# Expert sums straight from PSUM on VectorE, and inverse roots from ScalarE and VectorE instead of GpSimd's powers

## The reference

```
weights = softmax over the two best of x @ expert_embeddings.T
first 512 tokens of each expert's list are kept (capacity)
inter = relu(tokens_e @ first_linear[e].T)      # 512 x 256 -> 512 x 512
out   = inter @ second_linear[e].T * weight     # 512 x 512 -> 512 x 256
x     = layernorm(x + sum of both experts' out)
```

## Time and profile before

| | us |
|---|---|
| median of 3 runs (lowest, highest) | 1020.33 (1018.7, 1022.15) |
| the profiled execution's own time | 1013.04 |
| its span, first to last instruction | 1010.9 |
| PE busy in the span | 980.9 (97%) |
| DVE, ACT, POOL busy | 823.5, 724.2, 587.9 |

### The profile page before, as it was taken

How to read it: one execution, slowest core, us unless ns; L and a number is a source line. 1 busy time by engine, 2 the same in 40 slices (tenths; PEclk the granted TensorE clock), 3 DMA queues, 4 the chain that set the end, 5 groups by cost and what they waited for, 6 DMA issues and landing times.

```text
span 1010.9 us, 21647 instructions
## 1 busy us (share of the span) xinstructions
PE 980.9 (97%) x7018; PEld 928.6 (92%) x7018; DVE 823.5 (81%) x2087; ACT 724.2 (72%) x1857; POOL 587.9 (58%) x1069
## 2 busy tenths in 40 slices
PE   8999999999999999999999999999999999999993
PEld 6789999999999999999999999999999999889993
DVE  6887878888888888887888788878888887767774
ACT  6686877777787768786878677877777766547761
POOL 4743465665566656665575637565665464536786
PEclk9999999999999999999999999999999999999997
DMA  7663031112211131104110402031112213555542
GB/s 249 193 143 109 16 110 47 51 46 88 69 52 46 59 98 52 47 18 140 51 46 2 135 29 58 33 110 47 51 46 91 98 31 124 193 173 163 170 149 88
DMA packets 63030, 88.97 MB, mean 88 GB/s; under 512 B 15540, under 2 KB 44008, under 8 KB 62920
## 3 DMA queue, kind: packets, MB, share of 16 engines
q1 hardware_dynamic: 56968, 71.10, 22.8%
q0 software_dynamic: 5952, 16.50, 4.9%
HBM read 49.31 MB, written 38.26 MB: 87 GB/s over the span
## 4 chain that ended last, share of the span: by engine, by line
PE 79%; ACT 6%; DVE 6%; issue 4%; POOL 2%; DMA 1%; POOLq 0%; SPq 0%; DVEq 0%; ACTq 0%
PE ps L629 21%; PE ps L631 21%; PE ps L630 21%; PE ps L658 7%; PE ps L737 3%; DVE nmx L1838 2%; PE ps L673 1%; PE ps L675 1%; PE ps L775 1%; ACT hp L1094 1%; PE ps L768 1%; ACT prob L1251 1%; POOL out L2327 1%; PE ps L761 1%; DMA cxs<-in_ctxt 1%
## 5 line engine op out<-in xcount | busy, mean ns | idle before, releaser
L2212 POOL TENSOR_SCALAR prob<-prob,rinv 128x333 f32<-128x333 f32 x256 | 143.5, 572 | 234.5 <-DVE rinv L1847 234.0
L1246 ACT ACTIVATE oT_hi<-ps 128x256 fp32r<-128x256 f32 x126 | 48.4, 384 | 150.5 <-PE ps L675 150.5
L629 PE MATMUL ps<-kv_lo,w_hi 128*128 128x256 f32 (+1 forms) x512 | 154.9, 303 | 1.1 <-DVE kv_lo L1398 1.1
L631 PE MATMUL ps<-kv_hi,w_hi 128*128 128x256 f32 (+1 forms) x512 | 152.9, 299 | 0.0
L630 PE MATMUL ps<-kv_hi,w_lo 128*128 128x256 f32 (+1 forms) x512 | 152.5, 298 | 0.0
L1251 ACT ACTIVATE prob<-ps,nmx 128x333 f32<-128x333 f32 x256 | 134.8, 537 | 7.7 <-DVE nmx L1838 7.7
L1398 DVE TENSOR_TENSOR pT_lo<-ps,pT_hi 128x512 fp32r<-128x512 f32 x254 | 130.8, 549 | 0.9 <-ACT pT_hi L1263 0.3
L1838 DVE TENSOR_REDUCE nmx<-ps 128x2 f32<-128x666 f32 x128 | 108.4, 847 | 8.4 <-PE ps L631 7.0
L658 PE MATMUL ps<-ident,prob 128*128 128x128 f32 (+1 forms) x768 | 105.9, 273 | 1.8 <-POOL prob L2212 1.0
L629 PEld LDWEIGHTS ps<-kv_lo,w_hi 128*128 128x128 f32 x512 | 96.9, 189 | 1.7 <-issue 1.5
L631 PEld LDWEIGHTS ps<-kv_hi,w_hi 128*128 128x128 f32 x512 | 96.8, 189 | 0.0
(11 more groups left out here) (330 smaller groups left out, 3319.3 us busy)
## 6 DMA issues: line engine op xcount, KB each, us to landing
wraw<-in_W SPq DMA_DIRECT2D x14, 512.0 KB, 5.2
vcd_hi<-vst_hi SPq DMA_DIRECT2D x10, 512.0 KB, 2.7
vcd_lo<-vst_lo SPq DMA_DIRECT2D x10, 512.0 KB, 3.7
v_hi<-vcd_hi SPq DMA_DIRECT2D x32, 154.0 KB
v_lo<-vcd_hi SPq DMA_DIRECT2D x32, 154.0 KB
slots<-initr SPq DMA_DIRECT2D x8, 522.0 KB, 9.9
xs<-in_x SPq DMA_DIRECT2D x16, 256.0 KB, 4.3
xts<-in_xT SPq DMA_DIRECT2D x15, 256.0 KB, 4.0
```

Source lines behind the costliest of these rows:

```text
L629: pe.matmul(dst, hi1, lo2, start=first, stop=False, skip_group_check=True)
L631: return pe.matmul(dst, hi1, hi2, start=False, stop=last, skip_group_check=True)
L2212: pool.tensor_scalar(prob[:, h % 2, t, 0:KEYS], prob[:, h % 2, t, 0:KEYS], rinv[:, h % 2, t:t + 1], 1.0, ALU.mult, ALU.mult).then_inc(norm ...
```

## The change

1. The inverse roots of the expert norms leave POOL (`power` is gone). ACT takes a square root (`deviation`), DVE its reciprocal and one Newton step (`inverse`: four instructions, each of which waits for the one before). One Sqrt on a scratch tile is put at the end of ACT's `ending()`.
2. The results no longer pass through ACT (`result`, `result_tile` are gone): DVE reads PSUM, multiplies by the slot's weight and adds `bs` in one instruction a tile (`sum_of`); `z_set` counts tiles instead of halves, and PE waits for it in place of `yo_set` before it writes a bank again.
3. In ACT's loop `scale(e - 1)` stands in one piece, and `deviation` ahead of the fourth `relu` tile.
4. `block_moments` moves from ahead of `part1(1, 1)` to behind `weights(1, 1, 16)`, and `block_norm` from ahead of `xparts(1)` to behind `shift(0)` in the first round of the loop. SP's program keeps its order.
5. For the last sequence's norm POOL's power has 2 columns in place of 4, and DVE leaves out two small instructions (`residual_stats` returns early).

```diff
@@ sync
-                    keep_sums(e, slice(0, 2), 2 * e + 1)
-                    keep_sums(e, slice(2, 4), 2 * e + 2)
+                    keep_sums(e, slice(0, 2), 4 * e + 2)
+                    keep_sums(e, slice(2, 4), 4 * e + 4)
@@ tensor: outer, outer_tiles, last_outer
-                    need(pe, yo_set, 4 * e - 2 + 2 * pair)
+                    need(pe, z_set, 4 * e - 2 + 2 * pair)
@@ scalar
                 xparts(0)
+                act.activation(warm[:], warm[:], ACT.Sqrt)
...
+            def deviation(part, e, tiles):
+                act.wait_ge(fstat_set, 3 * part + 3)
+                act.activation(f_sd[:, e, tiles], f_vv[:, e, tiles], ACT.Sqrt).then_inc(fsd_set, 1)
...
-            result(0, 0, (0, 1))
             xparts(1)
-            result(0, 0, (2, 3))
             for e in range(1, E - 1):
                 u = e % 2
                 parts(e + 1, 1 - u)
-                relu(e)
+                relu(e, range(0, 3))
+                deviation(e - 1, e - 1, slice(0, ST))
+                relu(e, range(3, 4))
                 xparts(e + 1)
-                scale(e - 1, (0, 1), e - 1)
-                if e < E - 2:
-                    result(e, u, (0, 1))
-                    scale(e - 1, (2, 3), e - 1)
-                    result(e, u, (2, 3))
...
+                scale(e - 1, range(ST), e - 1)
...
             last_relu(1, (0, 1))
+            deviation(E - 2, E - 2, slice(0, 3))
+            deviation(E - 1, E - 2, slice(3, 4))
             scale(E - 2, T_ORDER[0:3], E - 2)
             scale(E - 2, T_ORDER[3:4], E - 1)
             last_relu(1, (2, 3))
+            deviation(E, E - 1, slice(0, 2))
+            deviation(E + 1, E - 1, slice(2, 4))
@@ vector
                 dve.tensor_scalar(c_vv[:, 0, :], c_mv[:, :, 1], 1.0, EPS, ALU.mult, ALU.add).then_inc(cstat_set, 1)
+                if at(b, B):
+                    return
...
+            def sum_of(e, s, bank):
+                u = e % 2
+                need(dve, z_st, PART + 32 * (e - 1))
+                need(dve, fo_set, 4 * (e - 1))
+                base_of(e, s // 2)
+                return dve.scalar_tensor_tensor(out=yo[u][:, s, :], in0=bank, scalar=wsl[:, e, s:s + 1],
+                                                in1=bs[u][:, s, 0:D], op0=ALU.mult, op1=ALU.add).then_inc(z_set, 1)
             def sums(e, half):
-                dve.wait_ge(yo_set, 4 * e + 2 * half + 2)
-                base_of(e, half)
-                dve.tensor_tensor(yo[u][:, o, :], yo[u][:, o, :], bs[u][:, o, 0:D], ALU.add).then_inc(z_set, 1)
+                dve.wait_ge(o_mm, 2 * e + half + 1)
+                dve.wait_ge(cols_set, 3 * e + 3)
+                for s in (2 * half, 2 * half + 1):
+                    sum_of(e, s, ps[:, 6 + half, (s % 2) * D:(s % 2 + 1) * D])
...
+            def inverse(part, e, tiles, steps):
+                o = (slice(None), e, tiles)
+                dve.wait_ge(fsd_set, part + 1)
+                dve.reciprocal(f_r0[o], f_sd[o]).then_inc(fnm_set, 1)
+                dve.wait_ge(fnm_set, steps + 1)
+                dve.scalar_tensor_tensor(out=f_cr[o], in0=f_r0[o], scalar=-0.5, in1=f_r0[o], op0=ALU.mult,
+                                         op1=ALU.mult).then_inc(fnm_set, 1)
+                dve.wait_ge(fnm_set, steps + 2)
+                dve.tensor_tensor(f_cr[o], f_cr[o], f_vv[o], ALU.mult).then_inc(fnm_set, 1)
+                dve.wait_ge(fnm_set, steps + 3)
+                dve.scalar_tensor_tensor(out=f_rs[o], in0=f_cr[o], scalar=1.5, in1=f_r0[o], op0=ALU.add,
+                                         op1=ALU.mult).then_inc(fnm_set, 1)
+                dve.wait_ge(fnm_set, steps + 4)
             def shift(part, e, tiles):
-                dve.wait_ge(frs_set, part + 1)
+                inverse(part, e, tiles, 5 * part)
...
             relu(0)
-            block_moments()
             part1(1, 1)
             dve.wait_ge(sc_done, 64 * B)
             part2(1, 1)
-            block_norm()
             xparts(1)
             weights(1, 1, 16)
+            block_moments()
             sums(0, 0)
             for e in range(1, E - 1):
...
                 shift(e - 1, e - 1, slice(0, ST))
+                if e == 1:
+                    block_norm()
                 xparts(e + 1)
@@ gpsimd
-                pool.wait_ge(cstat_set, 7 * B)
-                pool.tensor_tensor(c_rs[:].rearrange("p c t -> p (c t)"), c_vv[:].rearrange("p c t -> p (c t)"), powm[:],
-                                   ALU.pow).then_inc(crs_set, 1)
+                pool.wait_ge(cstat_set, 7 * B - 2)
+                pool.tensor_tensor(c_rs[:, 0, :], c_vv[:, 0, :], powm[:, 0:NT], ALU.pow).then_inc(crs_set, 1)
...
             for e in range(1, E - 1):
-                power(e - 1, e - 1, slice(0, ST))
                 gather(e)
                 finished(e - 1, range(ST))
-            power(E - 2, E - 2, slice(0, 3))
-            power(E - 1, E - 2, slice(3, 4))
             gather(E - 1)
-            finished(E - 2, (0, 1, 2), T_ORDER)
-            power(E, E - 1, slice(0, 2))
-            finished(E - 2, (3,), T_ORDER)
-            power(E + 1, E - 1, slice(2, 4))
+            finished(E - 2, range(ST), T_ORDER)
             finished(E - 1, range(ST))
```

More of the change, by code:

```diff
@@ L280, in build @@
         f_vv = s2("f_vv", [P, E, ST])
+        f_sd = s2("f_sd", [P, E, ST])
+        f_r0 = s2("f_r0", [P, E, ST])
+        f_cr = s2("f_cr", [P, E, ST])
         f_rs = s2("f_rs", [P, E, ST])
@@ L1009, in outer_tiles @@
                 for n, s in enumerate(T_ORDER):
-                    need(pe, yo_set, (4 * e - 2, 4 * e, 4 * e + 1, 4 * e + 2)[n])
+                    need(pe, z_set, (4 * e - 2, 4 * e, 4 * e + 1, 4 * e + 2)[n])
                     for i in range(I // P):
@@ L1043, in last_outer @@
                 if s < 2:
-                    need(pe, yo_set, 4 * e - 2 + 2 * s)
+                    need(pe, z_set, 4 * e - 2 + 2 * s)
                 for i in tiles:
@@ L1321, in _, with relu @@
             ending()
-            def relu(e):
-                for i in range(I // P):
+            def relu(e, tiles=range(I // P)):
+                for i in tiles:
                     need(act, h_mm, 4 * stage(e) + i + 1)
@@ L1328, in relu @@
                     act.activation(h_hi[:, i, :], ps[:, 2 + i, :], ACT.Relu).then_inc(hh_set, 1)
[L1330 to L1346, removed]
+            def deviation(part, e, tiles):
+                act.wait_ge(fstat_set, 3 * part + 3)
+                act.activation(f_sd[:, e, tiles], f_vv[:, e, tiles], ACT.Sqrt).then_inc(fsd_set, 1)
             def scale(e, tiles, part):
-                need(act, fnm_set, part + 1)
+                need(act, fnm_set, 5 * (part + 1))
                 need(act, sc_done, 64 * B + 64 * (e - 1))
@@ L1886, in base_of @@
                     dve.wait_ge(bs_ld[half], 32 * e)
+            def sum_of(e, s, bank):
[5 more added lines that the diff above has]
+                                                in1=bs[u][:, s, 0:D], op0=ALU.mult, op1=ALU.add).then_inc(z_set, 1)
             def sums(e, half):
[L1890 to L1893 removed]
+                dve.wait_ge(o_mm, 2 * e + half + 1)
+                dve.wait_ge(cols_set, 3 * e + 3)
+                for s in (2 * half, 2 * half + 1):
+                    sum_of(e, s, ps[:, 6 + half, (s % 2) * D:(s % 2 + 1) * D])
             def sum_tile(e, n):
[L1897 to L1902 removed]
+                s = T_ORDER[n]
+                dve.wait_ge(block_mm, 2 + n)
+                sum_of(e, s, ps[:, 6 + s // 2, (s % 2) * D:(s % 2 + 1) * D])
+                dve.wait_ge(z_set, 4 * e + n + 1)
+                return dve.bn_stats(f_st[:, e, s, :], yo[e % 2][:, s, :])
             def variance(part, e, tiles):
@@ L1913, in moments @@
             def moments(e):
-                dve.wait_ge(z_set, 2 * e + 2)
+                dve.wait_ge(z_set, 4 * e + 4)
                 for s in range(ST):
@@ L2062, in last_scale @@
                 e, u = E - 1, 1
-                dve.wait_ge(frs_set, part + 1)
+                inverse(part, e, slice(tiles[0], tiles[-1] + 1), 5 * E + 4 * (part - E))
                 dve.wait_ge(sc_done, 64 * B + 64 * (E - 2))
@@ L2298, in _ @@
             ending()
-            def power(part, e, tiles):
-                pool.wait_ge(fstat_set, 3 * part + 3)
-                n = len(range(ST)[tiles])
-                pool.tensor_tensor(f_rs[:, e, tiles], f_vv[:, e, tiles], powm[:, 0:n], ALU.pow).then_inc(frs_set, 1)
             def gather(e):
```

29 lines of the change are left out of this document (6 added, 23 removed).

## The result

| | before | after |
|---|---|---|
| median (lowest to highest), 7 runs each | 1022.15 (1018.7 to 1023.34) | 1034.1 (1028.07 to 1037.01) |
| ratio, with its 95% interval | | 1.0113 (1.0087 to 1.0139) |
| profiled execution, its span | 1013.04, 1010.9 | 1037.01, 1035.1 |

The change makes the kernel slower by 12 us. The forecast was +6.0 and 1026.3 us; 1034.1 lies above its range (1020 to 1030). Three later comparisons of the same two kernels, on three chips, gave 1.0066, 1.0059 and 1.0077 (+6.7, +6.3, +7.3 us; see the experiments). So the 12 us are two things: some 7 that the program cost on every later chip, and 5 that came in the first comparison alone.

A forecast was written before the change was run, and what follows sets the result against it. PE, busy 97%, was taken as the bound. Terms -0.45 - 0.3 + 7.5 - 0.2 - 0.7 gave +5.9, taken as +6.0: profiled 1013.04 to 1019.0, plus 7.3 to the median, 1026.3 us; range 1020 to 1030.

The forecast's parts named there:

- The order of SP's queue, and the stall: Late block_norm holds SP's store of lo, delaying gather(1); PE stalls 5.15 us before outer(2), +7.5 with the clock's fall.
- The clock fell: After the stall ahead of outer(2), the PE clock drops to half and 2.4 us are lost.
- w_lo(3): DVE's w_lo(3), done at 24.3 us after inner(1), is hidden behind outer(2) if the clock falls.
- The ring: DVE sums, SP store, POOL gather, next sums: 11.7 or 12.6 us an expert against PE's 12.18; +7.4 if it paces.
- Inner(1) and the last norm: Two savings: block work gone ahead of inner(1), -0.3; POOL's shorter power before the last norm's transposes, -0.45.
- The last part: Expert 6's end: DVE loses the ACT copy, gains the inverse and waits for a gather; -0.2 (-0.9 to +0.5).
- PE's new wait for z_set binds nothing of its own: PE's wait for DVE's sums before rewriting a bank costs nothing: sums(1, 0) are done when outer(2) is due.
- rival (a): The end gives it back: stall nearer 4.5, no clock fall, gather(7)'s pause gone; +1.4, 1021.7 us, chance 0.20.
- The end power: At the end, POOL's 0.74 us power ahead of expert 6's fourth store goes; -0.7.
- The pause in gather(7): POOL's 2.08 us pause after the first issue of expert 7's gather; kept in the forecast, other end -2.1.
- rival (b): POOL was the pace, so freeing it makes the last gathers early; -4.4, 1015.9 us, chance 0.11.
- From the profile to the median: The median stands 7.3 us above the profiled execution, and this difference carries over: 1019.0 becomes 1026.3.

The follow-up runs named there:

- e7: Changed kernel with PE doing the transposes of rows(3) six times over in the gap ahead of outer(2); ratio 1.0064 to the kernel before.
- e10: e9 with the transposes of rows(3) done six times over in the gap ahead of outer(2); 0.8 us below e9 by the medians.
- e8: The changed kernel once more, unchanged, on a later chip; ratio 1.0059 to the kernel before.
- e3: The changed kernel once more, unchanged, for a second trace; 1020.94 us, ratio 1.0066 to the kernel before.
- e2: Kernel before with only block_moments and block_norm moved as in the change, SP's order unchanged; median +6.0 us.
- e5: Kernel before with only the results taken from PSUM into the sums on DVE, for all experts; ratio 1.0000.
- e6: Kernel before with only Sqrt on ACT and the Newton step on DVE replacing POOL's powers; ratio 0.9995, -0.7 us by the medians.
- e14: The changed kernel, unchanged, on a further chip; ratio 1.0077 to the kernel before.
- e9: Changed kernel with ACT's copy of the result back for expert 6 alone, SP's store of lo left as changed; 1.65 us below e8 by the medians.
- e4: Changed kernel with SP's store of lo behind expert 0's sums and ACT's result copy back for expert 6; ratio 0.9970 to the kernel before.
- e13: e4 again, unchanged, on another chip; ratio 0.9976 to the kernel before.
- e1: Changed kernel with SP's store of lo moved behind expert 0's stores of sums and expert 3's token load; ratio 0.9989 to the kernel before.
- e12: e4 without the Newton step, POOL's powers back for every expert; 2.3 us above e13 on the same chip.
- e11: Changed kernel with SP's store of lo behind expert 0's sums and results left as ACT's copies for every expert; ratio 0.9981 to the kernel before.

## Why the prediction was half right

**The order of SP's queue, and the stall.** Right in every step. From inner(1)'s end (916.87) gather(1) started after 8.1 us (7.7 forecast), the last sum was done after 15.6 (15.5), outer(2) began after 18.4 (18.2). The stall was 5.2 to 5.6 in four traces (5.15). The clock fell, and outer(2) took 8.1 in the first trace against 5.65, the 2.4 forecast; against e7 and e10, which kept the clock, it cost 1.5 to 2.1. The term as a whole was +7.5; the stages of e8 and e3 are 7.55 and 7.76 longer than before. That the sum fits so well is partly luck: without the fall the stages are 6.5 to 6.6 longer (e10, e7) and not 5.7, and the fall adds 1.0 to 1.7 to them and not 1.8. w_lo(3) was done at 941.3, behind outer(2)'s start and ahead of its end: hidden, as said.

**The ring.** A toss between 11.7 and 12.6 us. The collisions came (issues of 1.58 and 1.55 in e8, each begun some 0.5 after w_lo), but the stages of e8 behind the stall are 12.23, 11.92 and 12.18 apart: PE's own pace.

**Inner(1) and the last norm.** The stage between the transposes of experts 1 and 2 is 0.4 shorter wherever part 4 of the change is in, e2 included (9.27 to 9.37 against 9.71), and not in e5 and e6, which lack it (9.71 and 9.70); -0.3 was forecast. PE's wait ahead of the last norm's transposes fell from 0.65 to 0.18 (-0.45 forecast). What that is worth in the time is not shown: the transposes of rows(1) start at 905.51 before and between 904.87 and 907.44 in the other traces, with this part and without it.

**The last part: the step that failed.** It is the sentence "PE's new wait for z_set binds nothing of its own" and with it the term "-0.2 (-0.9 to +0.5)". I had worked that wait out for the round of expert 2 and not for outer_tiles(6), where the bank is wanted again half an outer later, while DVE has w_lo(7) ahead of the sum. PE waited 2.94 us there. The term measured +2.05 in e3, e8 and e14 (12.82 less 10.77), all of it by a second fall of the clock: e7, with the same wait and the clock kept, is at 10.52. e9 takes it back. In e5, with the new sums alone, PE waited 2.14 us there and the median showed no cost; the term belongs to the whole program. With it the span of e8 splits as -0.4 + 7.55 + 2.05 - 0.8 = +8.4, which is 1019.3 - 1010.9; that is a division of one pair of traces, not a proof. The price of rival (a), an end that gives something back, had the wrong sign.

**The end power.** -0.7 forecast. The last stretch is 0.4 to 0.8 shorter than before in e3, e8 and e14, but it varies by more than that: 24.1 to 25.2 in the four traces with the power (mean 24.5), 23.3 to 24.7 in the eleven without it (mean 23.8, the first trace left out). That agrees with -0.7 and doesn't show it. The pause in gather(7), 2.08 to 2.13, is in every trace, with POOL's powers and without them: it does not go with them, and rival (b) loses its 2.1.

**Rival (b), POOL as the pace**, was put at -4.4 if expert 1's gather is not late. With the store moved and the bank given back in time, e4 and e13 stand at 0.9970 and 0.9976 (-3.2 and -2.6 us), and 2.3 of that hang on the powers; with the powers alone taken out (e6) it was 0.7, not clear of zero. So rival (b) had a sound part, smaller than its -4.4, and SP's order covered it.

**From the profile to the median.** The forecast carried the 7.3 us between the profiled execution and the median over unchanged. On the four later chips that distance was 0.6 to 1.3. There the changed kernel costs +6.3 to +7.3 by the medians. That this is near the +6.0 is luck in part, since two errors cancel. The profiled execution of e8 stands 8.1 above that of the kernel before, which is more than forecast by about the missing term; but the one before lies 1.3 below the median on that chip and e8's 0.5 above its own, and 8.1 - 1.3 - 0.5 = 6.3.

**What took the time out of the range, and stays open.** 1034.1 is 7.8 above the forecast. 1.8 of it is the kernel before, whose median was 1022.15 and not 1020.33 in this comparison; some 0.8 is what the program costs above +6.0 on the later chips; the other 5 are of the first comparison alone. With the failed term alone the forecast would have been 1028.4, within the range: it is the 5 us that lead out of it. The forecast had no term for them. They go with late starts that no other trace shows, and the kernel before was 8 us slower there too than anywhere else, so that the place or the hour may have to do with it. Why the changed kernel suffers more was not found; the cause stays open. Open too is why the clock fell in outer(6) of e8 and not in the same wait of e7.

## A version that beats both

e4_copy_six, on two chips (e4 and e13): 0.9970 (0.9961 to 0.9979) and 0.9976 (0.9966 to 0.9986) of the kernel before, a small gain of some 3 us but clear of zero both times, and some 10 us below the changed one (e13 and e14, on one chip). It keeps the roots on ACT and DVE, moves SP's store of lo behind the sums of expert 0, and leaves ACT the copy where a bank is wanted back soon.

## What to carry to other kernels

When an instruction is moved to a later place, look up who waits for its result, and what stands behind that waiter in its queue: here a store of 0.4 us cost 7.5. When one engine takes over another's read of PSUM, the read inherits the new engine's queue; go through every place where PE wants that bank again, not only through the usual round. And price a stop of PE with the clock behind it, which in outer(6) was worth more than the wait (2.3 against 0.3 to 0.5), but did not come in every execution.

## What the runs showed of the hardware

- The fall of the clock does not go by the length of the stop alone. Worked out from the mean of the stretch in which it fell, it came 2.9 us (e8), 3.3 (first trace, e3) and 4.3 (e9) after the start of the stop ahead of outer(2), 2.0 into the stop of 2.94 in outer(6) in e8, and not at all in the same stop of e7. It can also come when PE is already at work again: 0.4 us behind the stop of 3.20 in e1, and 0.6 behind the one of 2.14 in e5.
- In e4 and e8 every issue of a gather that began while DVE worked on w_lo ended some 0.3 us before w_lo did: one begun 0.05 after w_lo's start took 1.98 us (e4), those begun 0.45 and 0.49 after it took 1.58 and 1.55 (e8), where most others take 0.95. In e12 one of them ended later (1.96 us, begun at 931.01), so this is no rule without exceptions.
- Between the end of the last sum and the start of the gather that waits for its store lay 2.6 (before) to 4.0 us (e11), for the same store in the same place.
- In the first trace of the changed kernel waits of DVE and ACT on PE ended 3.7 us and more after PE's last matmul.
